# Attention in bursts of three units, value matmuls of 256 queries on all four column tiles

## The chip, the cores and the metric

The kernel runs on one core of one Trainium2 chip. The metric is the device time of one execution in microseconds. The kernel before took 1284.57 us (median of three runs, 1284.06 to 1284.71).

## What is computed

A transformer block on x of shape (4, 1024, 256), in fp32. First attention with 16 heads of 16 channels:

```python
q, k, v = (split_heads(binlinear(layernorm(x), W, b)) for W, b in ((Wq, bq), (Wk, bk), (Wv, bv)))
att = softmax(einsum('bhtd,bhsd->bhts', q, k) * 16 ** -0.5)
y = einsum('bhts,bhsd->bhtd', att, v)
x = x + layernorm(binlinear(y.reshape(B, T, C), Wp, bp))
```

where binlinear multiplies by sign(W) and the mean of |W| over a row. Then a feed-forward part with ternary weights: silu(x w1) * (x w2), two hidden layers of 1024 with gelu, and a last layer back to 256, again with a layer norm and a residual. The change is in the attention alone.

## The kernel before

The program has three stages, each a block in which every engine has its own instruction list: project (queries, keys and values of batch 0), attention, and tail_ffn. The queries, keys and values go through DRAM scratch.

attention goes over four batches. A quad is four heads; a batch has four quads (QUADS_OF_BATCH), and each quad is done in two blocks of 512 queries (BLK), called halves here: 32 halves in all (HALVES). A half has eight turns (ST = 8), one for every 128 keys, so a batch has 64 turns (TURNS_OF_BATCH) and the kernel 256.

In a turn TensorE (block.tensor) does two units, one for each pair of heads. scores(turn), line 1040, writes a unit in two matmuls, one for each head: 50 rows by 128 keys as weights, 512 queries moving, in fp32r. The two lie on different halves of the array's rows. A unit fills one of three PSUM tiles s_ps (two banks each); unit a may be written only when the exp of unit a - 3 is done (line 1051, semaphore probs_ready). ScalarE (line 1202) turns a unit of scores, 128 x 1024, into probs with one exp, line 1210, and signals probs_ready; it needs the semaphore scored for its input and, for the first unit of a turn, pv_done for the buffer (there are 2 x 2 buffers probs). pv(turn), line 1058, multiplies by the values in full fp32: four matmuls, one for each head, each with 17 columns of weights (16 channels and a column of ones, which gives the sum of the softmax), all 512 queries moving, on column tile j of the array (tile_position=(0, 32 * j)). The profile shows a fp32 matmul as two weight loads and two matmul records. All turns of a half accumulate in one bank, y_ps. TensorE's order is scores of turn t, values of turn t - 1, and then, at certain turns, a piece of the next batch's projection.

These pieces are placed by projected(b, t), line 1125. A batch has two windows of 28 turns, from turn 4 and turn 32; r is the turn within a window. At r = 3 and 4 there are four transposes each (turn_x, line 1071), at r = 6, 9, 12 and 15 four matmuls of 512 columns each (project_qk, line 1083, lines 1089 and 1090), at r = 17 and 19 eight of 256 columns each (project_v), at r = 21 four of 512 columns in bf16 (sum_squares), and in the second window two tiny matmuls at r = 23 and 25. All of them go through one bank, p_ps, which VectorE reads. In the last batch prepared(t), line 1174, has two pieces of eight matmuls, two of four transposes and a small one instead. At the start of each batch there is a read of a flag and a branch (lines 1183 to 1188).

At the end of a half VectorE copies y_ps to y_sb (copy_y, line 1231, 512 elements a partition); the first value matmul of the next half waits for it (line 1064). SyncE then stores y_sb with one DMA (store_y, line 878, issued at line 882) and, every second half, issues the loads of the quad after next. The stores' semaphores y_stored are waited for by SyncE, ScalarE and VectorE at the start of tail_ffn. VectorE also does the projection's vector work and checks the feed-forward weights (check_w) in the same list, in turn order.

Of the kernel before, what the change touches and what calls it, by code (L numbers as in the profile page):

```python
# [6 lines left out]
F32 = mybir.dt.float32  # L7
# [3 lines left out]
ACT = mybir.ActivationFunctionType  # L11
# [3 lines left out]
P = 128  # L15
BATCH, SEQ, DIM = 4, 1024, 256
# [3 lines left out]
BLK = 512  # L20
# [5 lines left out]
QUAD = 4  # L26
QUADS = BATCH * HEADS // QUAD
ST = SEQ // P
QROWS = QUAD * HEAD_DIM
VCOLS = HEAD_DIM + 1  # L30
VQUAD = QUAD * VCOLS
HALF = 64
PAIRS = QUAD // 2
STACK = 3 * HEAD_DIM
STACK_M = STACK + 2
ONES_FROM = 32
QUADS_OF_BATCH = HEADS // QUAD
BATCH_BLOCKS = SEQ // BLK
HALVES = QUADS * BATCH_BLOCKS
TURNS_OF_BATCH = QUADS_OF_BATCH * BATCH_BLOCKS * ST  # L40
FIRST_WINDOW, WINDOW = 4, 28
AT_NORM, AT_TURN, AT_QK, AT_V, AT_SUM, AT_TOP, AT_SPREAD = 2, (3, 4), (6, 9, 12, 15), (17, 19), 21, 23, 25
EPS = 1e-5
SCALE = HEAD_DIM ** -0.5
# [667 lines left out]
def attention(nc, const, q_scr, k_scr, v_scr, m_scr, y_scr, ffn_w, w_scr, W, quads, x, tail_in):  # L712
# [6 lines left out]
    q_st, k_st, v_st, loaded, stored = quads.q, quads.k, quads.v, quads.loaded, quads.stored  # L719
# [5 lines left out]
    with ExitStack() as ctx:  # L725
        def sb(name, shape, dt):
            return ctx.enter_context(nc.sbuf_tensor(name, shape, dt))
# [4 lines left out]
        N = QUAD * ST  # L732
        UNITS_OF_BATCH = PAIRS * TURNS_OF_BATCH
        TURNS = BATCH * TURNS_OF_BATCH
# [15 lines left out]
        half = sb("half", [1, 1], F32)  # L750
# [1 line left out]
        shift_col = sb("shift_col", [HEADS, 1], F32)  # L752
        row_bits = sb("row_bits", [P, 1], F32)
        top_bits = sb("top_bits", [1, 1], F32)
        probs = [[sb(f"probs{w}{pp}", [P, 2, BLK], F32) for pp in range(PAIRS)] for w in range(2)]
        y_sb = [sb(f"y_sb{u}", [P, BLK], F32) for u in range(2)]
        qk = [sb(f"pj_qk{u}", [P, BLK], F32) for u in range(2)]
        square = sb("pj_square", [P, QK, BLK], BF16)
# [1 line left out]
        s_ps = [ctx.enter_context(nc.psum_tensor(f"s_ps{i}", [P, 2, BLK], F32)) for i in range(3)]  # L760
        y_ps = ctx.enter_context(nc.psum_tensor("y_ps", [P, BLK], F32))
# [8 lines left out]
        scored = sem("scored")  # L770
        probs_ready = sem("probs_ready")
        pv_done = sem("pv_done")
        y_copied = sem("y_copied")
        y_cleared = sem("y_cleared")
        y_stored = tail_in.y_stored
# [67 lines left out]
        def _(sp):  # L843
# [34 lines left out]
            def store_y(n):  # L878

                g, tb = divmod(n, BATCH_BLOCKS)  # L880
                sp.wait_ge(y_copied, n + 1)
                sp.dma_start(y_scr[g * P:(g + 1) * P, tb * BLK:(tb + 1) * BLK], y_sb[tb][:, :])\
                    .then_inc(y_stored[tb], 16)

            def load_xb(n):

# [57 lines left out]
            for b in range(BATCH):  # L944
# [11 lines left out]
                for t in range(TURNS_OF_BATCH):  # L956
                    turn = b * TURNS_OF_BATCH + t
                    if turn and turn % ST == 0:
                        n = turn // ST - 1
                        store_y(n)  # L960
                        g = n // BATCH_BLOCKS + 2
# [57 lines left out]
        def _(pe):  # L1019
# [17 lines left out]
                pe.wait_ge(mx_loaded[b], 16 * (12 * (QUADS_OF_BATCH + 1) + 2))  # L1037
                pe.wait_ge(mx_split[b], 3 * QUADS_OF_BATCH + 1)

            def scores(turn):  # L1040

                n, s = divmod(turn, ST)
                g, tb = divmod(n, BATCH_BLOCKS)
                u = g % 2
                if s == 0 and tb == 0:
                    pe.wait_ge(loaded[u], 16 * QUAD_LOADS * (g // 2 + 1))
                    pe.wait_ge(m_loaded[u], 16 * 2 * (g // 2 + 1))
                for pp in range(PAIRS):
                    a = PAIRS * turn + pp
                    if a >= 3:  # L1050
                        pe.wait_ge(probs_ready, a - 2)
                    for hh in range(2):
                        rows = slice(hh * HALF, hh * HALF + STACK_M)
                        i = pe.matmul(s_ps[a % 3][:, hh, :], k_st[u][rows, pp, s * P:(s + 1) * P],  # L1054
                                      q_st[u][rows, pp, tb * BLK:(tb + 1) * BLK], start=True, stop=True)
                    i.then_inc(scored, 1)

            def pv(turn):

                n, s = divmod(turn, ST)  # L1060
                g = n // BATCH_BLOCKS
                pe.wait_ge(probs_ready, PAIRS * (turn + 1))
                if s == 0 and n:
                    pe.wait_ge(y_copied, n)
                for j in range(QUAD):
                    i = pe.matmul(y_ps[32 * j:32 * j + VCOLS, :], v_st[g % 2][:, s, VCOLS * j:VCOLS * (j + 1)],  # L1066
                                  probs[turn % 2][j // 2][:, j % 2, :],
                                  start=(s == 0), stop=(s == ST - 1), tile_position=(0, 32 * j))
                i.then_inc(pv_done, 1)

            def turn_x(b, u, n, c):
# [53 lines left out]
            def projected(b, t):  # L1125

                u, r = window(t)
                n = BATCH_BLOCKS * (b - 1) + u
                for c in range(CT):
                    if r == AT_TURN[c]:  # L1130
                        turn_x(b, u, n, c)
                    if r == AT_V[c]:
                        project_v(n, c)
                for m in range(QK):
                    if r == AT_QK[m]:
                        project_qk(n, m)
                if r == AT_SUM:
                    sum_squares(n)
                if u == BATCH_BLOCKS - 1:
                    if r == AT_TOP:  # L1140
                        turn_top(b)
                    if r == AT_SPREAD:
                        spread_bound(b)
# [30 lines left out]
            def prepared(t):  # L1174

                if t in (36, 38):
                    project_y((t - 36) // 2)
                if t in (51, 53):
                    turn_x1((t - 51) // 2)
                if t == 57:  # L1180
                    turn_bits()

            for b in range(BATCH):
                if b:
                    pe.wait_ge(flag_set, b)
                wide = pe.value_load(const.wide_range[:, b:b + 1], min_val=0, max_val=1)
                with pe.If(wide):
                    most_of_rows(b)
                if b == 0:
                    pe.wait_ge(y_cleared, 1)  # L1190
                for t in range(TURNS_OF_BATCH):
                    turn = b * TURNS_OF_BATCH + t
                    scores(turn)
                    if turn:
                        pv(turn - 1)
                    if b + 1 < BATCH:
                        projected(b + 1, t)
                    else:
                        prepared(t)
            pv(TURNS - 1)  # L1200

        @block.scalar
        def _(act):
            for turn in range(TURNS):
                if turn >= 2:
                    act.wait_ge(pv_done, turn - 1)
                for pp in range(PAIRS):
                    a = PAIRS * turn + pp
                    act.wait_ge(scored, a + 1)
                    act.activation(probs[turn % 2][pp][:, :, :], s_ps[a % 3][:, :, :], ACT.Exp,  # L1210
                                   scale=SCALE).then_inc(probs_ready, 1)

        @block.vector
        def _(dve):
# [14 lines left out]
                                      ALU.subtract).then_inc(mx_split[b], 1)  # L1229

            def copy_y(n):
                dve.wait_ge(pv_done, ST * (n + 1))
                if n >= 2:
                    dve.wait_ge(y_stored[n % 2], 16 * (n // 2))
                dve.tensor_copy(y_sb[n % 2][:, :], y_ps[:, :]).then_inc(y_copied, 1)  # L1235

            def check_w(i):
# [164 lines left out]
            for b in range(BATCH):  # L1402
# [5 lines left out]
                for t in range(TURNS_OF_BATCH):  # L1408
                    turn = b * TURNS_OF_BATCH + t
# [13 lines left out]
def tail_ffn(nc, x, y_scr, const, W, tail_in, out):  # L1423
# [9 lines left out]
    with ExitStack() as ctx:  # L1433
        def sb(name, shape, dt):
            return ctx.enter_context(nc.sbuf_tensor(name, shape, dt))
# [110 lines left out]
        @block.sync  # L1546
        def _(sp):
            def load_y(t, b, u):

                sp.wait_ge(y_lo_done, t)  # L1550
                load_tail_y(sp, y_scr, tail_in, b, u)

            def load_x(t, u):
                if not isinstance(t, int) or t >= 2:
                    sp.wait_ge(o_done, t - 1)
                sp.dma_start(x1[u][:, :, :], x_blk[t]).then_inc(x_loaded[u], 16)

            def store(f):
                sp.wait_ge(o_done, f + 1)
                sp.dma_start(o_blk[f], o_sb[:, :, :]).then_inc(o_stored, 16)  # L1560

            def step(i, u, ahead, behind):
                if ahead:
                    load_y(i + 1, *ahead)
                if behind:
                    store(i - 1)
                if ahead:
                    load_x(i + 1, 1 - u)

            for u in range(2):  # L1570
                sp.wait_ge(tail_in.y_stored[u], 16 * HALVES // 2)
            blocks(sp, step, lambda: store(BLOCKS - 1))
            sp.wait_ge(o_stored, 16 * BLOCKS)

# [91 lines left out]
        def _(act):  # L1666
# [54 lines left out]
                ln_std(ln_out(BLOCKS - 1))  # L1721

            for u in range(2):
                act.wait_ge(tail_in.y_stored[u], 16 * HALVES // 2)
            blocks(act, step, end)

        @block.vector
        def _(dve):
# [114 lines left out]
                scale_out(i, ahead)  # L1843

            for u in range(2):
                dve.wait_ge(tail_in.y_stored[u], 16 * HALVES // 2)
            blocks(dve, step, lambda: finish_out(BLOCKS - 1, (BLOCKS - 1) % 2))


# [33 lines left out]
```

## Time and profile before

| | us |
|---|---|
| median of three runs | 1284.57 |
| lowest, highest | 1284.06, 1284.71 |
| the profiled execution, whole | 1285.64 |
| its span, first to last instruction | 1283.9 |
| TensorE busy (share of the span) | 1193.3 (93%) |
| ScalarE busy | 726.2 (57%) |
| VectorE busy | 631.1 (49%) |
| attention, first exp start to last exp start | 65.2 to 593.8 |
| granted TensorE clock, mean share | 0.983 |

The span is divided into the start and the projection of batch 0 (to 65 us), attention (to 598), and the feed-forward part (to 1283.9). Busy means that some instruction of the engine was under way. A matmul's record begins when it starts to stream and ends about 165 ns after its columns have gone through, so that records overlap and TensorE looks busy where it is only draining.

### The profile page before, as it was taken

What the parts mean: (1) busy time and instruction counts of PE and PEld (TensorE: products, weight loads), DVE (VectorE), ACT (ScalarE), POOL (GpSimd) and SP (SyncE); (2) the same over time, 40 slices, a digit from 0 to 9 for tenths busy, and PEclk for the clock granted to TensorE, in tenths of its full rate; (3) what the DMA queues carried; (4) which work ended last, traced back from release to release, by engine and by line L of the source; (5) the groups of instructions that cost most, each with busy time, mean ns of one, the idle gap of its engine ahead of it and who ended that gap; (6) DMA issues with size and microseconds to landing.
All of it is one profiled execution on the core that took longest, in us unless ns stands there. A gap on an engine that the chain in (4) does not pass through costs nothing.

```text
span 1283.9 us, 17482 instructions
## 1 busy us (share of the span) xinstructions
PE 1193.3 (93%) x6705; PEld 727.1 (57%) x6705; DVE 631.1 (49%) x1150; ACT 726.2 (57%) x866; POOL 78.6 (6%) x78
## 2 busy tenths in 40 slices
PE   3299989999999999998999999999999999999997
PEld 3123222323232322224888888888888888888886
DVE  6234433444353431442656747646577376575523
ACT  4288979898989899997324224233242342432411
POOL 5101110111011100000000000000000000000000
PEclk9689999999999999999999999999999999999999
DMA  3868567776765678512010201001001010010000
GB/s 114 225 175 229 132 158 160 181 183 165 153 173 158 195 162 156 89 33 66 1 34 1 66 1 34 33 1 41 26 14 53 1 34 33 1 33 1 17 1 17
DMA packets 52712, 107.55 MB, mean 84 GB/s; under 512 B 6544, under 2 KB 23312, under 8 KB 52620
## 3 DMA queue, kind: packets, MB, share of 16 engines
q1 hardware_dynamic: 52332, 105.54, 32.5%
q10 hardware_dynamic: 288, 0.79, 0.5%
q8 instruction: 57, 0.93, 0.3%
q14 instruction: 35, 0.29, 0.1%
HBM read 71.94 MB, written 45.88 MB: 92 GB/s over the span
## 4 chain that ended last, share of the span: by engine, by line
PE 53%; DVE 0%; issue 0%; ACT 0%; POOLq 0%; DVEq 0%
PE ffn_ps L1601 23%; PE ffn_ps L1600 23%; PE ffn_ps L1628 2%; PE ffn_ps L1629 2%; PE side_ps L1584 1%; PE side_ps L1593 0%; DVE ln_stats L1731 0%; DVE zn L1742 0%; DVE zn L1783 0%; DVE zn L1793 0%; DVE ln_mean_var L1735 0%; ACT ln_std L1669 0%; DVE ln_rstd L1739 0%; POOLq L1538 0%; DVEq L1781 0%
## 5 line engine op out<-in xcount | busy, mean ns | idle before, releaser
L1210 ACT ACTIVATE probs<-s_ps 128x1024 f32<-128x1024 f32 x512 | 477.0, 1054 | 71.9 <-PE s_ps L1054 71.6
L1601 PE MATMUL ffn_ps<-h_lo,W 128*128 128x512 f32 x1024 | 405.9, 396 | 0.0
L1600 PE MATMUL ffn_ps<-h_hi,W 128*128 128x512 f32 x1024 | 403.0, 394 | 0.0
L1066 PE MATMUL y_ps<-probs,v_st 128*17 128x512 f32 x2048 | 272.0, 603 | 34.1 <-ACT probs L1210 17.2
L1601 PEld LDWEIGHTS ffn_ps<-h_lo,W 128*128 128x128 f32 x1024 | 192.0, 188 | 47.5
L1600 PEld LDWEIGHTS ffn_ps<-h_hi,W 128*128 128x128 f32 x1024 | 191.9, 187 | 45.7
L1690 ACT ACTIVATE hid<-ffn_ps,scales 128x512 f32<-128x512 f32 x128 | 80.9, 685 | 240.0 <-PE ffn_ps L1601 235.0
L1054 PE MATMUL s_ps<-q_st,k_st 50*128 50x512 f32 x1024 | 190.0, 449 | 20.3 <-DMA q_st<-shift 19.6
L1054 PEld LDWEIGHTS s_ps<-q_st,k_st 50*128 50x128 f32 x1024 | 77.5, 187 | 200.4 <-ACT probs L1210 163.1
L1807 DVE CAST h_hi<-hid 128x512 fp32r<-128x512 f32 x128 | 53.4, 417 | 192.8 <-ACT hid L1690 192.7
L1801 DVE TENSOR_TENSOR h_lo<-hid,h_hi 128x512 fp32r<-128x512 f32 x192 | 130.0, 684 | 1.1
L1066 PEld LDWEIGHTS y_ps<-probs,v_st 128*17 128x17 f32 x2048 | 34.7, 95 | 141.3 <-ACT probs L1210 120.0
L1600 PE MATMUL ffn_ps<-x_hi,W 128*128 128x512 f32 x256 | 100.7, 393 | 2.7 <-POOLq L1538 2.7
L1601 PE MATMUL ffn_ps<-x_lo,W 128*128 128x512 f32 x256 | 100.4, 392 | 0.0
L1235 DVE COPY y_sb<-y_ps 128x512 f32<-128x512 f32 x32 | 22.1, 690 | 145.7 <-PE y_ps L1066 145.7
L1815 DVE SCALAR_TENSOR_TENSOR hid<-ffn_ps,scales,gate 128x512 f32<-128x512 f32 x64 | 47.5, 750 | 43.7 <-ACT gate L1701 26.3
L1701 ACT ACTIVATE gate<-ffn_ps,scales 128x512 f32<-128x512 f32 x64 | 43.3, 687 | 32.8 <-PE ffn_ps L1601 32.8
L1628 PE MATMUL ffn_ps<-W,h_hi 128*128 128x256 f32 x256 | 61.6, 283 | 0.0
L1629 PE MATMUL ffn_ps<-W,h_lo 128*128 128x256 f32 x256 | 61.0, 281 | 0.0
L1669 ACT ACTIVATE ln_std<-ln_mean_var,eps 128x4 f32<-128x4 f32 x22 | 6.5, 298 | 88.0 <-DVE ln_mean_var L1735 88.0
L1600 PEld LDWEIGHTS ffn_ps<-x_hi,W 128*128 128x128 f32 x256 | 48.6, 190 | 13.5 <-POOLq L1538 3.6
L142 DVE RECIPROCAL sums<-sums 128x256 f32<-128x256 f32 x32 | 54.5, 1730 | 0.0
(156 smaller groups left out, 944.8 us busy)
## 6 DMA issues: line engine op xcount, KB each, us to landing
q_st<-q_scr SPq DMA_DIRECT2D x96, 128.0 KB, 7.4
k_st<-k_scr SPq DMA_DIRECT2D x90, 128.0 KB, 4.6
w_scr<-ffn_w SPq DMA_DIRECT2D x16, 704.0 KB, 7.8
W<-w_scr SPq DMA_DIRECT2D x16, 704.0 KB, 6.2
y_scr<-y_sb SPq DMA_DIRECT2D x32, 256.0 KB, 2.2
v_st<-v_scr SPq DMA_DIRECT2D x16, 272.0 KB, 8.7
y<-y_scr SPq DMA_DIRECT2D x16, 256.0 KB
sums<-y_scr SPq DMA_DIRECT2D x16, 256.0 KB
```

What stands on the lines that cost most here:

```text
L142: dve.reciprocal(sums, sums).then_inc(tail_in.inverted, 1)
L1054: i = pe.matmul(s_ps[a % 3][:, hh, :], k_st[u][rows, pp, s * P:(s + 1) * P], q_st[u][rows, pp, tb * BLK:(tb + 1) * BLK], start=True, stop= ...
L1066: i = pe.matmul(y_ps[32 * j:32 * j + VCOLS, :], v_st[g % 2][:, s, VCOLS * j:VCOLS * (j + 1)], probs[turn % 2][j // 2][:, j % 2, :], start= ...
L1210: act.activation(probs[turn % 2][pp][:, :, :], s_ps[a % 3][:, :, :], ACT.Exp, scale=SCALE).then_inc(probs_ready, 1)
L1600: pe.matmul(bank_of(t)[:, :], w, hi[:, k, :].bitcast(form), start=(k == 0), stop=False)
L1601: mm = pe.matmul(bank_of(t)[:, :], w, lo[:, k, :].bitcast(form), start=False, stop=last)
L1628: pe.matmul(dst, hi[:, k, tokens].bitcast(form), w, start=(k == 0 and a == 0), stop=False)
L1629: mm = pe.matmul(dst, lo[:, k, tokens].bitcast(form), w, start=False, stop=(k == HT - 1 and a == per_bank - 1))
L1690: act.activation(hid[n % 3][:, :], bank_of(t)[:, :], ACT.Gelu, scale=scales[:, s:s + 1]).then_inc(gelu_done, 1)
L1801: dve.tensor_tensor(h_lo[a][:, n, :], hid[n % 3][:, :], h_hi[a][:, n, :].bitcast(F32), ALU.subtract).then_inc(h_lo_done, 1)
L1807: dve.tensor_copy(h_hi[a][:, n, :], hid[n % 3][:, :]).then_inc(hi2_done, 1)
L1815: dve.scalar_tensor_tensor(hid[n % 3][:, :], bank_of(2 * n + 1)[:, :], scales[:, S2_AT + n:S2_AT + n + 1], gate[n % 3][:, :], ALU.mult, AL ...
```

## The change

Units are counted through, without regard to turns. A half has 16 units, in bursts of 3, 3, 3, 3, 2 and 2. TensorE's order is now: scores of a burst, values of the burst before it, and then the pieces of projection of every turn that this burst's scores complete. pv takes one unit: a head's 512 queries are split in two halves of 256, and the four pairs of head and query half lie on the four column tiles. So y_ps has another layout: rows are head of the pair and query half, columns are the pair and 256 queries; one y_sb needs four stores to keep the layout in DRAM. There are five buffers probs, one for each unit, in place of four. ScalarE waits for pv_done and scored at every unit.

```diff
+BURSTS = (3, 3, 3, 3, 2, 2)
+UNITS_OF_HALF = 2 * ST
+PROBS = 5
+QH = BLK // 2
...
-                sp.dma_start(y_scr[g * P:(g + 1) * P, tb * BLK:(tb + 1) * BLK], y_sb[tb][:, :])\
-                    .then_inc(y_stored[tb], 16)
+                for j in range(2):
+                    for h in range(2):
+                        c = 32 * (2 * j + h)
+                        sp.dma_start(rows[j, h], y_sb[tb][c:c + 32, :].rearrange("d (pp q) -> d pp q", pp=PAIRS))\
+                            .then_inc(y_stored[tb], 16)
...
-                pe.wait_ge(probs_ready, PAIRS * (turn + 1))
-                if s == 0 and n:
+                pe.wait_ge(probs_ready, a + 1)
+                if s == 0 and pp == 0 and n:
                     pe.wait_ge(y_copied, n)
-                for j in range(QUAD):
-                    i = pe.matmul(y_ps[32 * j:32 * j + VCOLS, :], v_st[g % 2][:, s, VCOLS * j:VCOLS * (j + 1)],
-                                  probs[turn % 2][j // 2][:, j % 2, :],
-                                  start=(s == 0), stop=(s == ST - 1), tile_position=(0, 32 * j))
+                for c in range(QUAD):
+                    j, h = divmod(c, 2)
+                    head = PAIRS * pp + j
+                    i = pe.matmul(y_ps[32 * c:32 * c + VCOLS, pp * QH:(pp + 1) * QH],
+                                  v_st[g % 2][:, s, VCOLS * head:VCOLS * (head + 1)],
+                                  probs[a % PROBS][:, j, h * QH:(h + 1) * QH],
+                                  start=(s == 0 and pp == 0), stop=(s == ST - 1 and pp == PAIRS - 1), tile_position=(0, 32 * c))
...
+                for half in range(QUADS_OF_BATCH * BATCH_BLOCKS):
+                    for k, size in enumerate(BURSTS):
+                        a = b * UNITS_OF_BATCH + half * UNITS_OF_HALF + sum(BURSTS[:k])
+                        for i in range(a, a + size):
+                            scores(i)
+                        for i in range(max(a - BURSTS[k - 1], 0), a):
+                            pv(i)
+                        while t < TURNS_OF_BATCH and PAIRS * (b * TURNS_OF_BATCH + t + 1) <= a + size:
+                            if b + 1 < BATCH:
+                                projected(b + 1, t)
+                            else:
+                                prepared(t)
+                            t += 1
...
+            for a in range(PAIRS * TURNS):
+                if a >= PROBS:
+                    act.wait_ge(pv_done, a - PROBS + 1)
+                act.wait_ge(scored, a + 1)
+                act.activation(probs[a % PROBS][:, :, :], s_ps[a % 3][:, :, :], ACT.Exp, scale=SCALE)\
+                    .then_inc(probs_ready, 1)
```

The waits on y_stored in tail_ffn and in copy_y count four stores a half. VectorE's and GpSimd's lists are otherwise as before.

## Rows read from the trace of the kernel before

**Rows 1.** The page: busy time of each engine over the whole span.

```profile
PE 1193.3 (93%) x6705; PEld 727.1 (57%) x6705; DVE 631.1 (49%) x1150; ACT 726.2 (57%) x866; POOL 78.6 (6%) x78
```

**Rows 2.** Stretches (batches 0, 1, 3, end): busy PE, PEld, DVE, ACT, POOL; clock, DMA, GB/s.

```profile
65.00:204.80 139.80, 130.14 (x855) 40.50 (x851) 51.38 (x87) 119.82 (x129) 17.68 (x15) 0.96 0.66 170
204.80:339.40 134.60, 126.35 (x861) 39.75 (x860) 57.27 (x96) 119.57 (x129) 18.18 (x15) 1.00 0.72 174
...
474.00:594.00 120.00, 112.21 (x790) 30.38 (x789) 36.45 (x62) 117.18 (x128) 2.43 (x4) 1.00 0.46 85
594.00:598.60 4.60, 1.22 (x12) 0.13 (x8) 0.69 (x1) 0.89 (x1) 0.00 (x0) 0.97 0.15 57
```

**Rows 3.** The page: costliest groups by line (busy us, mean ns, idle before).

```profile
L1210 ACT ACTIVATE probs<-s_ps 128x1024 f32<-128x1024 f32 x512 | 477.0, 1054 | 71.9 <-PE s_ps L1054 71.6
L1066 PE MATMUL y_ps<-probs,v_st 128*17 128x512 f32 x2048 | 272.0, 603 | 34.1 <-ACT probs L1210 17.2
```

**Rows 4.** Waits, 60 to 598 us: waiter, waited for, total us, times, longest.

```profile
ACT probs L1210 <- PE s_ps L1054: 71.6, 61, 19.2
```

**Rows 5.** Timeline of a turn without projection: start us, length us, engine, line.

```profile
589.89 0.61 PE L1066 MATMUL y_ps<-probs,v_st 128*17 128x512 f32 x4
590.43 0.73 PE L1054 MATMUL s_ps<-q_st,k_st 50*128 50x512 f32 x4
591.28 1.05 PE L1066 MATMUL y_ps<-probs,v_st 128*17 128x512 f32 x8
```

**Rows 6.** Timeline of ScalarE alone: the last twelve exps, and one of them.

```profile
583.79 11.10 ACT L1210 ACTIVATE probs<-s_ps 128x1024 f32<-128x1024 f32 x12
...
589.23 1.08 ACT L1210 ACTIVATE probs<-s_ps 128x1024 f32<-128x1024 f32 x1
```

**Rows 7.** Timeline around one project_qk in batch 1.

```profile
302.07 2.88 ACT L1210 ACTIVATE probs<-s_ps 128x1024 f32<-128x1024 f32 x3
...
303.17 1.05 PE L1066 MATMUL y_ps<-probs,v_st 128*17 128x512 f32 x8
...
304.15 0.50 PE L1089 MATMUL p_ps<-x_hi,signs 128*128 128x512 f32 x1
...
304.95 0.40 PE L1090 MATMUL p_ps<-x_lo,signs 128*128 128x512 f32 x1
...
305.28 0.73 PE L1054 MATMUL s_ps<-q_st,k_st 50*128 50x512 f32 x4
...
305.89 1.02 ACT L1210 ACTIVATE probs<-s_ps 128x1024 f32<-128x1024 f32 x1 [0.94 <-PE s_ps L1054]
...
305.94 1.05 PE L1066 MATMUL y_ps<-probs,v_st 128*17 128x512 f32 x7
```

**Rows 8.** Timeline of 2 ns, 337.550 to 337.552 us: what of a pv had started.

```profile
337.54 0.11 PEld L1066 LDWEIGHTS y_ps<-probs,v_st 128*17 128x17 f32 x4 [0.55 <-ACT probs L1210]
337.54 0.62 PE L1066 MATMUL y_ps<-probs,v_st 128*17 128x512 f32 x3
```

**Rows 9.** Timeline after the branch at the start of batch 2.

```profile
338.71 0.33 PEld L1054 LDWEIGHTS s_ps<-q_st,k_st 50*128 50x128 f32 x4 [1.04 <-issue]
...
339.40 0.13 PEld L1066 LDWEIGHTS y_ps<-probs,v_st 128*17 128x17 f32 x8 [0.36 <-ACT probs L1210]
```

**Rows 10.** Timelines of VectorE and TensorE at the latest copy of batch 1.

```profile
308.03 0.68 DVE L1235 COPY y_sb<-y_ps 128x512 f32<-128x512 f32 x1
...
308.85 1.05 PE L1066 MATMUL y_ps<-probs,v_st 128*17 128x512 f32 x8 [1.20 <-ACT probs L1210]
```

**Rows 11.** Timeline of the end of attention.

```profile
594.95 1.05 PE L1066 MATMUL y_ps<-probs,v_st 128*17 128x512 f32 x8 [0.78 <-ACT probs L1210]
...
596.78 0.33 SPq L882 DMA_DIRECT2D y_scr<-y_sb  x1
```

**Rows 12.** Timeline of SyncE's queue: two stores issued in a row.

```profile
301.59 0.33 SPq L896 DMA_DIRECT2D k_scr<-y  x1
301.97 0.43 SPq L896 DMA_DIRECT2D k_scr<-sums  x1
```

More of the change, by code:

```diff
@@ L754, in attention @@
         top_bits = sb("top_bits", [1, 1], F32)
-        probs = [[sb(f"probs{w}{pp}", [P, 2, BLK], F32) for pp in range(PAIRS)] for w in range(2)]
+        probs = [sb(f"probs{i}", [P, 2, BLK], F32) for i in range(PROBS)]
         y_sb = [sb(f"y_sb{u}", [P, BLK], F32) for u in range(2)]
@@ L881, in store_y @@
                 sp.wait_ge(y_copied, n + 1)
-                sp.dma_start(y_scr[g * P:(g + 1) * P, tb * BLK:(tb + 1) * BLK], y_sb[tb][:, :])\
-                    .then_inc(y_stored[tb], 16)
+                rows = y_scr[g * P:(g + 1) * P, tb * BLK:(tb + 1) * BLK].rearrange("(pp j d) (h q) -> j h d pp q", pp=PAIRS,
+                                                                                   j=2, h=2)
+                for j in range(2):
[3 more added lines that the diff above has]
+                            .then_inc(y_stored[tb], 16)
             def load_xb(n):
@@ L1038, in most_of_rows, with scores @@
                 pe.wait_ge(mx_split[b], 3 * QUADS_OF_BATCH + 1)
-            def scores(turn):
-                n, s = divmod(turn, ST)
+            def scores(a):
+                n, s = divmod(a // PAIRS, ST)
+                pp = a % PAIRS
                 g, tb = divmod(n, BATCH_BLOCKS)
                 u = g % 2
-                if s == 0 and tb == 0:
+                if s == 0 and tb == 0 and pp == 0:
                     pe.wait_ge(loaded[u], 16 * QUAD_LOADS * (g // 2 + 1))
                     pe.wait_ge(m_loaded[u], 16 * 2 * (g // 2 + 1))
[L1048 to L1056, printed above, removed]
@@ L1058, in pv @@
-            def pv(turn):
-                n, s = divmod(turn, ST)
+                if a >= 3:
+                    pe.wait_ge(probs_ready, a - 2)
+                for hh in range(2):
+                    rows = slice(hh * HALF, hh * HALF + STACK_M)
+                    i = pe.matmul(s_ps[a % 3][:, hh, :], k_st[u][rows, pp, s * P:(s + 1) * P],
+                                  q_st[u][rows, pp, tb * BLK:(tb + 1) * BLK], start=True, stop=True)
+                i.then_inc(scored, 1)
+            def pv(a):
+                n, s = divmod(a // PAIRS, ST)
+                pp = a % PAIRS
@@ L1190, in _ @@
                     pe.wait_ge(y_cleared, 1)
[L1191 to L1200, printed above, removed]
+                t = 0
+                for half in range(QUADS_OF_BATCH * BATCH_BLOCKS):
[11 more added lines that the diff above has]
+                            t += 1
+            for i in range(PAIRS * TURNS - BURSTS[-1], PAIRS * TURNS):
+                pv(i)
         @block.scalar
         def _(act):
[L1204 to L1211, printed above, removed]
+            for a in range(PAIRS * TURNS):
[4 more added lines that the diff above has]
+                    .then_inc(probs_ready, 1)
         @block.vector
@@ L1231, in copy_y @@
             def copy_y(n):
-                dve.wait_ge(pv_done, ST * (n + 1))
+                dve.wait_ge(pv_done, UNITS_OF_HALF * (n + 1))
                 if n >= 2:
-                    dve.wait_ge(y_stored[n % 2], 16 * (n // 2))
+                    dve.wait_ge(y_stored[n % 2], 16 * QUAD * (n // 2))
                 dve.tensor_copy(y_sb[n % 2][:, :], y_ps[:, :]).then_inc(y_copied, 1)
@@ L1570, in _ @@
             for u in range(2):
-                sp.wait_ge(tail_in.y_stored[u], 16 * HALVES // 2)
+                sp.wait_ge(tail_in.y_stored[u], 16 * QUAD * HALVES // 2)
             blocks(sp, step, lambda: store(BLOCKS - 1))
@@ L1723, in _ @@
             for u in range(2):
-                act.wait_ge(tail_in.y_stored[u], 16 * HALVES // 2)
+                act.wait_ge(tail_in.y_stored[u], 16 * QUAD * HALVES // 2)
             blocks(act, step, end)
@@ L1845, in _ @@
             for u in range(2):
-                dve.wait_ge(tail_in.y_stored[u], 16 * HALVES // 2)
+                dve.wait_ge(tail_in.y_stored[u], 16 * QUAD * HALVES // 2)
             blocks(dve, step, lambda: finish_out(BLOCKS - 1, (BLOCKS - 1) % 2))
```

## The prediction, made before the changed kernel ran

> **What bounds the kernel now.** I read the busy times first [rows 1], then the stretches [rows 2]: the change can only act in attention, 65 to 598 us, 42% of the span. There TensorE looks busiest, but its records overlap while it drains; ScalarE is the engine to follow. In batch 3, which has few pieces of projection, ScalarE is busy 117.2 of 120.0 us; in batch 1 it is busy 119.6 of 134.6 [rows 2]. Its floor: the last twelve exps end at 594.89 and the one that starts at 589.23 ends at 590.31, so the five behind it took 4.58, a pitch of 0.916 us [rows 6]; 16 units (a half) 14.66, 128 units (a batch) 117.3. Batch 1 loses 17.3 us above that floor, batch 0 about 22, batch 3 about 3. The waits name the cause: ScalarE waited for scores 61 times, 71.6 us, 19.2 of them before the first exp [rows 3, 4].
>
> Why it waits is a chain. From the end of a turn's second exp: 0.05 to the value matmuls [rows 6, 11]; 0.98 to TensorE's next work, of which 0.44 is the first group of four (1.05 less 0.61), 0.54 the second with the switch [rows 5, 7]; 0.61 to the start of the exp; 1.02 for it [rows 7]. That is 2.66, and ScalarE allows three pitches, 2.75: 0.09 of slack. A project_qk lies between 304.15 and 305.28, 1.13 us, and the next exp ends 1.96 after the one before it instead of 0.92: 1.04 is lost, 1.13 less the slack [rows 7]. So nearly the whole of each piece of projection becomes idle time of ScalarE, though TensorE itself needs only 0.66 + 0.98 = 1.64 of a turn's 1.83 [rows 7].
>
> **The durations of the changed order.** A score unit streams 0.23: the four projection matmuls start 0.80 apart in all, the first pitch 0.34 with its weight load open (0.73 less 0.40 gives it too), the others 0.23 [rows 7]. From the second unit to the values it is 0.66 - 0.34 = 0.32. So three units of scores take 0.34 + 0.23 + 0.32 = 0.89, two 0.66. A value group streams 0.427 (0.44 less 0.013 for the first load); a unit of 256 queries is two groups of half that, 0.427 again, with the switch and first load 0.13 once for a burst: 1.41 for three units, 0.98 for two. That no time is lost between one unit's groups and the next's the trace of before never shows, as a tile there has two groups and no more. The bounds are nothing, and the nearest price of an opened load and switch, 0.09 (0.32 less 0.23). I take nothing: the second group's loads start in the shadow of the first's stream, and within 10 ns four loads and three matmuls had begun [rows 8], so that a load held back lets those of the other tiles pass; from the second unit on there are 0.21 us of stream to hide a load in.
>
> TensorE's pace by bursts is then 0.89 + 0.98 = 1.87 (first), 2.30 (second to fourth), 0.66 + 1.41 = 2.07 (fifth), 1.64 (sixth); ScalarE's 2.75 four times and 1.83 twice. Over a half that is 12.5 against 13.1 before: two pairs of switches fewer.
>
> **The sum.** Where a chain binds, the steps from the end of an exp are: burst of three after three, 0.05 + 0.43 (last score unit with its load) + 1.41 + 0.61 + 1.02 = 3.52 against four pitches 3.67, slack 0.15. First after the sixth: 0.43 less, slack 0.58. To the sixth burst (unit 14) from unit 8: 0.05 + 0.43 + 1.41 + 0.66 + 1.40 + 0.61 + 1.02 = 5.58 against six pitches 5.50: it comes 0.07 to 0.09 late in every quiet half, a cost of the change of 32 x 0.07 = 2.2.
>
> A piece of 1.13 (project_qk; project_v is as long) lost 1.04 before. After: 0.54 behind the first burst; 0.97 behind the second and third; behind the fourth 0.97 and again 0.22 at unit 14 (2.07 against 1.83); 0.68 in place of 0.97 where it comes one burst after another piece, since nothing waits any more and the pace counts (2.30 + 1.13 - 2.75); 1.35 behind the fifth; 0.92 behind the sixth. Turn t of eight lies at burst 1 (t = 0), 2 (1, 2), 3 (3), 4 (4, 5), 5 (6), 6 (7). For the twelve pieces at turns 10, 13, 16, 19, 21, 23, 38, 41, 44, 47, 49 and 51 this gives 0.97 + 1.19 + 0.54 + 0.97 + 0.89 + 0.93 + 1.35 + 0.97 + 1.19 + 0.92 + 0.97 + 0.67 = 11.6 against 12.5: -0.9 for a batch. The first pair of transposes lost 0.9 and loses 0.44, as one falls behind the first burst; the second pair 0.9 and 0.8; the two sums of squares 1.5 and 1.3; the small matmuls 0.26 and 0.10: another -0.9. (Laid out unit by unit with these durations, attention before comes to 528.1 from first to last exp, where the trace has 528.6.)
>
> Then the copy of y. Before, the first value matmul of a half has it barely in time, and where VectorE is behind with the projection it waits: copy at 308.03, values at 308.85 after 1.20 idle [rows 10]. I put that at 1.0 for this half, 1.8 for one half of batch 0, and 0.03 to 0.2 for the others: 1.1 in batches 1 and 2. After, three more score units lie ahead of it: from the end of the exp of unit 15, 0.05 + 0.43 + 0.98 + 0.24 + 0.68 + 0.07 = 2.45 to the copy's end, and the matmul is due at 2.75 + 0.05 + 0.43 = 3.23, 0.8 of slack. All but 0.5 in batch 0 and 0.5 in batch 2 goes.
>
> Batch 1: -0.9 - 0.9 - 1.1 + 0.2 (its quiet halves) = -2.7. Batch 2: -2.3. Batch 0: -4.1, and -1.0 for its late copy, after which part of the clock's 4% shortfall [rows 2] falls, which the shorter wait should spare. Batch 3: 0.3 of late copies saved, 0.5 of late sixth bursts added: +0.2. Attention: -9.9.
>
> The end: three more stores are issued between the copy and the end of SyncE's list, 0.38 each [rows 12]: +1.1 (the first issue stands at 596.78 [rows 11]); but behind the last exp only one value unit of 0.54 is left instead of 0.98 [rows 11]: -0.4. Elsewhere the 31 x 3 extra issues lie in SyncE's list ahead of quad loads that are due a half or more later (14.7 us): nothing; without that cover 1.1 for each half with loads, 14 in all. ScalarE's extra waits are for pv(a - 5), done in the burst before: unit a + 2 of a burst wants the first value unit of the last one, ready 0.5 ahead. Nothing. TensorE's value instructions double to 16 a unit; its list must deliver 60 in 2.30 us, 38 ns each. After the branch, with an empty list, 20 (four loads, four matmuls, then eight loads and the four matmuls beside them) were there within 0.73 us, waits included [rows 9], so at most 36 ns each: nothing, but close.
>
> Sum, on the profiled execution (1285.64, span 1283.9) and equally on the median 1.1 below it: -9.9 + 0.7 = -9.2; 1284.57 - 9.2 = 1275.4.
>
> **Rules of the skill.** The rows show 0.11 of switch from values to scores (0.54 less 0.43) [rows 5]. The Trainium skill (TensorEngine Tiling (Array Packing), Key Properties) says that a change of tiling mode drains TensorE, which is why fewer changes should pay; row and rule agree. Against the change: the rows show loads of the same four tiles beginning while matmuls stream [rows 8]. The Trainium skill (TensorE: Matmul & The Clock Gate, Part 3, The mechanism) says that loads overlap matmuls in flight only where their row groups differ; here all four tiles take all rows, so by it every group would wait for its load. The trace speaks against it for two groups; for the third it can't.
>
> **Rivals.** *Loads come into the open between units.* 0.09 for every unit but a burst's first, 320 in all. In the bursts of three this turns 0.15 of slack into -0.03, and the way to unit 14, which has none, takes 0.37 more; with the losses at insertions 0.56 a half, 18 in all: 1293.4. It decides from about 0.05 a unit, where the gain is gone. If every group pays, 5 x 0.09 in a burst of three, less its slack, 1.2 a half, 39 in all: 1314. For it: no tile ever had a third group. Against it: rows 8. Chances 0.13 and 0.08.
>
> *The list of TensorE is too slow.* At 55 ns an instruction, half again the bound of rows 9, a burst of three takes 3.3 against 2.75, +20% in 469 us (512 exps): 1370. Against it rows 9. Chance 0.04.
>
> *The switches are saved and the time isn't.* The score unit that must wait still opens its load, each value group costs its 0.013, the slack is then what it was, and the late unit 14 is 0.2 later (32 x 0.2 = 6.4): -9.9 + 6.4 + 0.7 = -2.8, 1281.8. Half of its 0.17 lies on either side of the bound below.
>
> *More comes back than slack.* The pieces are spread by TensorE's spare time of 0.6 us a half, 32 x 0.6 = 20 at most: 1265. Chance 0.03.
>
> **How the numbers follow.** My forecast, 1275.4 (own range 1270 to 1280.5), has 0.55. The range to 1294 takes in the small gain and the milder rival, and leaves out the two dear ones and the tails; the low end is 1268. A difference under 0.2% (2.6 us) can't be told from none by these measurements. Faster: 0.55 + 0.08 + 0.03 = 0.66; within: 0.09; slower: 0.13 + 0.08 + 0.04 = 0.25.
>
> **What would show it.** Right: the exps at 0.916 in quiet halves with one 0.98 to 1.0 at unit 14; value groups 0.21 apart right through a burst; a lone project_qk costing 0.97 behind the second burst and 0.54 behind the first; batch 1 near 132; the last exp near 584. Wrong: a step of 0.3 instead of 0.21 between a unit's last group and the next unit's first; groups of a tile starting staggered; ScalarE waiting for probs buffers; the passage to the feed-forward part longer than 5.5 us.

## The result and the profile after

The changed kernel takes 1288.9 us (median; the kernel before, run beside it, 1284.8): a ratio of 1.0028, with a 95% interval of 1.0018 to 1.0038. It is slower by 0.3%, where 1275.4 us was forecast, 0.7% faster. The profiled execution took 1291.6 us with a span of 1289.8, 5.9 above that of before. Inside the batches the forecast gain comes, as the runs below show; at three places that the prediction never looked at, the starts of batches 1 to 3, it is all given back and more.

The page of the changed kernel, busy times and groups as in [rows 1, 3]:

```profile
PE 1195.0 (93%) x8753; PEld 803.9 (62%) x8753; DVE 631.0 (49%) x1150; ACT 728.8 (57%) x866; POOL 78.6 (6%) x78
...
L1226 ACT ACTIVATE probs<-s_ps 128x1024 f32<-128x1024 f32 x512 | 479.5, 1051 | 74.3 <-PE s_ps L1062 72.1
...
L1077 PE MATMUL y_ps<-probs,v_st 128*17 128x256 f32 x4096 | 263.6, 387 | 0.7 <-DVE y_sb L1251 0.4
```

TensorE's idle time before value matmuls fell from 34.1 us, of which 17.2 were waits for exps [rows 3], to 0.7. The waiting for exps is not gone: it stands before the score matmuls now, 24.8 us where it was 0.3. It costs nothing in itself, since ScalarE sets the pace. But ScalarE waits for scores as long as before, 72.1 us, and the waits say what is new in that. Those of the changed kernel, 60 to 604 us, columns as in [rows 4]:

```profile
ACT probs L1226 <- PE s_ps L1062: 72.1, 62, 18.8
...
PE s_ps L1062 <- ACT probs L1226: 24.8, 82, 0.4
...
PE s_ps L1062 <- DMA q_st<-m_scr: 11.9, 3, 4.8
```

TensorE waits three times, 11.9 us in all, for the load of rows from m_scr into q_st. Of the 71.6 us in [rows 4], 19.2 came before the first exp, and most of the rest were pieces of projection. Here 12 us are something else. The stretches by batch (columns as in [rows 2]; the bounds follow the changed kernel's own batches) show where:

```profile
65.00:204.00 139.00, 127.63 (x1359) 59.36 (x1355) 51.36 (x87) 120.40 (x129) 17.68 (x15) 0.97 0.70 172
204.00:339.60 135.60, 127.18 (x1374) 59.16 (x1371) 57.30 (x96) 120.10 (x129) 18.18 (x15) 0.98 0.71 173
339.60:477.40 137.80, 126.68 (x1375) 59.06 (x1371) 57.30 (x96) 120.17 (x129) 18.18 (x15) 0.98 0.69 167
477.40:600.00 122.60, 115.40 (x1315) 49.33 (x1315) 36.45 (x62) 118.72 (x128) 2.44 (x4) 0.98 0.47 83
```

Batch 1 takes 135.6 in place of 134.6, batch 3 122.6 in place of about 121; and the granted clock, 1.00 in batches 1 and 3 before [rows 2], is 0.98. One passage from a batch to the next, batch 0 to 1, is enough to see both. The timeline of the changed kernel (start us, length us, engine, line):

```profile
187.34 2.44 SPq L891 DMA_DIRECT2D y_scr<-y_sb  x4
...
188.88 0.20 PE L1135 MATMUL p_ps<-pj_bound,pj_ones 1*16 1x1 f32 x2
...
189.29 0.68 DVE L1339 CAST shift<-shift_col 16x1024 fp32r<-16x1024 f32 x1
...
191.33 0.34 SPq L178 DMA_DIRECT2D v_st<-v_scr  x1
191.72 0.43 SPq L877 DMA_DIRECT2D W<-w_scr  x1
192.20 0.52 SPq L872 DMA_DIRECT2D w_scr<-ffn_w  x1
...
192.76 0.58 SPq L915 DMA_DIRECT2D m_scr<-shift  x1
...
197.10 1.06 PE L1077 MATMUL y_ps<-probs,v_st 128*17 128x256 f32 x16
200.56 0.56 SPq L852 DMA_DIRECT2D q_st<-m_scr  x2
...
202.93 1.65 PE L1062 MATMUL s_ps<-q_st,k_st 50*128 50x512 f32 x6 [4.76 <-DMA q_st<-m_scr]
```

A batch's shift (a constant taken off the scores so that the exp can't overflow) is made at turn 57 of the batch before: a small matmul at 188.88, ready in SBUF at 189.97. It goes to DRAM and comes back as two rows of the first quad's query tile. Its store is issued at 192.76, behind four stores of y, a load of values that waits until the values are stored, and a piece of the feed-forward weights, 704 KB out and 704 KB in. It lands at 200.56, when SyncE goes on to the loads; these land at 202.9. TensorE had ended the batch's last values at about 198.2 and stood for 4.8 us. The same list in the kernel before:

```profile
191.00 0.43 SPq L174 DMA_DIRECT2D v_st<-v_scr  x1
191.47 0.46 SPq L873 DMA_DIRECT2D W<-w_scr  x1
191.97 0.50 SPq L868 DMA_DIRECT2D w_scr<-ffn_w  x1
192.81 0.98 SPq L906 DMA_DIRECT2D m_scr<-shift  x1
198.73 0.56 SPq L848 DMA_DIRECT2D q_st<-m_scr  x2
```

There the store landed at 198.73; with 2.4 for the loads as above (an estimate) the rows were in place at 201.1, and the next batch's scores came at 204.15. Three us of slack stood there that no view shows as a wait. The changed kernel comes 5.7 us earlier to this place and its store lands 1.8 later.

At the three passages ScalarE loses 4.9, 2.4 and 5.0 us, 12.3 together, reckoned as the distance between the ends of a batch's last exp and of the next batch's first, less the pitch of 0.916. These three are called the stalls from here on.

Around the end of each stall, and for some us behind it, TensorE runs at half its clock (1.2 of 2.4 GHz). A part of that stretch at the first stall, with the clock as the third number from the end:

```profile
203.00:206.80 3.80, 3.80 (x24) 1.74 (x26) 0.32 (x1) 2.85 (x3) 0.00 (x0) 0.50 0.00 0
```

### The profile page after: what moved, and what is told of

Read it like the earlier page. It is cut to its first block, busy times and chain, and to the rows that moved or that the text cites. A ratio compares the mean times of both kernels' runs of the same rounds, so it can differ in the third digit from the quotient of the medians.

```text
span 1289.8 us, 21927 instructions
## 1 busy us (share of the span) xinstructions
PE 1195.0 (93%) x8753; PEld 803.9 (62%) x8753; DVE 631.0 (49%) x1150; ACT 728.8 (57%) x866; POOL 78.6 (6%) x78
## 4 chain that ended last, share of the span: by engine, by line
PE 52%; DVE 0%; issue 0%; ACT 0%; POOLq 0%; DVEq 0%
PE ffn_ps L1617 23%; PE ffn_ps L1616 23%; PE ffn_ps L1644 2%; PE ffn_ps L1645 2%; PE side_ps L1600 1%; PE side_ps L1609 0%; DVE ln_stats L1747 0%; DVE zn L1758 0%; DVE zn L1799 0%; DVE zn L1809 0%; DVE ln_mean_var L1751 0%; ACT ln_std L1685 0%; DVE ln_rstd L1755 0%; POOLq L1554 0%; DVEq L1797 0%
## 5 line engine op out<-in xcount | busy, mean ns | idle before, releaser
L1226 ACT ACTIVATE probs<-s_ps 128x1024 f32<-128x1024 f32 x512 | 479.5, 1051 | 74.3 <-PE s_ps L1062 72.1
L1077 PE MATMUL y_ps<-probs,v_st 128*17 128x256 f32 x4096 | 263.6, 387 | 0.7 <-DVE y_sb L1251 0.4
L1062 PE MATMUL s_ps<-q_st,k_st 50*128 50x512 f32 x1024 | 203.8, 466 | 56.7 <-ACT probs L1226 24.8
L1062 PEld LDWEIGHTS s_ps<-q_st,k_st 50*128 50x128 f32 x1024 | 87.0, 190 | 169.4 <-ACT probs L1226 105.7
L1077 PEld LDWEIGHTS y_ps<-probs,v_st 128*17 128x17 f32 x4096 | 101.7, 98 | 128.2 <-issue 51.2
L1617 PEld LDWEIGHTS ffn_ps<-x_lo,W 128*128 128x128 f32 x256 | 48.6, 190 | 10.0
```

The costliest lines, as they stand in the source:

```text
L1077: i = pe.matmul(y_ps[32 * c:32 * c + VCOLS, pp * QH:(pp + 1) * QH], v_st[g % 2][:, s, VCOLS * head:VCOLS * (head + 1)], probs[a % PROBS][: ...
L1226: act.activation(probs[a % PROBS][:, :, :], s_ps[a % 3][:, :, :], ACT.Exp, scale=SCALE)\
L1617: mm = pe.matmul(bank_of(t)[:, :], w, lo[:, k, :].bitcast(form), start=False, stop=last)
```

## What was run to settle it

Every ratio below is to the kernel before as it ran beside the run in question. Its median was 1285.8 us beside e1 to e4 and again beside e5 to e8, 1284.8 beside the changed kernel; so a difference of 1 or 2 us between absolute times from different groups says little.

**The wait taken out (e1).** The first quad of a batch takes the shift rows of the batch before, which lie in DRAM long since, and loads them early. The softmax doesn't change with the shift as long as nothing overflows. What this kernel leaves out is each batch's own shift for its first quad. (Not shown below: load_shift itself, which now takes as a third argument the quad whose rows it reads.)

```diff
...
@@ def load_first_quad(b)
                 load_stacks(sp, q_scr, k_scr, q_st[0], k_st[0], b * QUADS_OF_BATCH, loaded[0])
+                load_shift(b * QUADS_OF_BATCH, m_loaded[0], (b - 1) * QUADS_OF_BATCH)
@@ def projected(b, t)
                     if r == AT_SPREAD + 2:
                         store_shift(b)
-                        sp.wait_ge(shift_stored, 16 * (b + 1))
-                        load_shift(b * QUADS_OF_BATCH, m_loaded[0])
@@ the loop over turns
                             load_quad(sp, q_scr, k_scr, v_scr, quads, g, g % 2)
+                            sp.wait_ge(shift_stored, 16 * (g // QUADS_OF_BATCH + 1))
                             load_shift(g, m_loaded[g % 2])
```

> The changed kernel, but the shift rows of a batch's first quad are not the ones computed for that batch: they are loaded early from the rows of the batch before (the softmax doesn't depend on the shift as long as nothing overflows), so that no wait for the shift's way through DRAM stands at the start of a batch. Theory A (the bursts gain what was forecast inside the batches, and the starts of batches 1 to 3 give it back, since the loads of the shift rows now end last): the three stalls of 4.9, 2.4 and 5.0 us before a batch's first exp go, and most of the 3.0 us that TensorE loses at its half clock behind them, together 12 to 15 us: 1274 to 1277, a ratio to the kernel before of 0.992 to 0.994. Theory B (the batches' starts wait for something else too, the quad's queries, keys and values or the rest of the queue): the stalls shrink by less than half, 1283 or more.

Measured: 1277.3 us, 0.9948 of the kernel before (0.993 to 0.9965), 11.6 under the changed kernel (10.3 by the two ratios). Theory A gave 1274 to 1277, of which this is 0.3 short; theory B's 1283 is out. No wait for m_scr is left, and ScalarE's waits for scores are 14 us shorter:

```profile
ACT probs L1227 <- PE s_ps L1063: 58.1, 55, 18.7
```

**The same edit on the kernel before (e2).**

> The kernel before with the same edit (a batch's first quad takes the shift rows of the batch before, loaded early). Theory A: before, the shift rows landed some 3 us ahead of TensorE, so nothing is won: within 1 us of the kernel before. Theory B, if the shift's way cost the kernel before something as well, by the traffic at the end of a batch: 3 us or more faster.

Measured: 1284.7, a ratio of 0.9994 (0.9976 to 1.0011). As theory A has it: before the change this way through DRAM cost nothing that shows (the interval reaches from 3 us faster to 1.4 slower). The stall isn't a fault of the kernel before that the change merely failed to mend; the change turned slack into a wait.

**What held the store back (e4).** Each batch's own shift again, and only the order in SyncE's list changed: weights behind shift.

```diff
-                    if turn % 13 == 4 and turn // 13 < QUADS:
-                        load_w(turn // 13)
+                    late = TURNS_OF_BATCH - 2
+                    due = [i for i in range(QUADS) if (13 * i + 4 == turn and t < 54)
+                           or (t == late and turn - late + 54 <= 13 * i + 4 <= turn + 1)]
+                    for i in due:
+                        load_w(i)
```

> The changed kernel with one thing moved: the copy of a piece of the feed-forward weights (704 KB to DRAM scratch and 704 KB from it) that SyncE issues just ahead of the store of the shift rows, at turns 56 to 58 of a batch, is issued at turn 62, behind the loads of the shift rows. Theory A in its sharper form (the shift rows are late because their store lies behind those 1.4 MB in the DMA queues): the store lands some 2 to 3 us after its issue in place of 7.8, the stalls at the starts of batches fall to under 1 us each, 1276 to 1280. If the lateness comes from SyncE's order instead (the four stores of y and the wait for the stored values ahead of it): the stalls shrink by 2 us at most, 1284 or more.

Measured: 1277.05, a ratio of 0.9943 (0.9922 to 0.9965): as good as leaving the wait out. SyncE's list at the same passage:

```profile
190.56 0.34 SPq L178 DMA_DIRECT2D v_st<-v_scr  x1
190.95 0.43 SPq L915 DMA_DIRECT2D m_scr<-shift  x1
193.62 0.56 SPq L852 DMA_DIRECT2D q_st<-m_scr  x2
194.23 0.35 SPq L877 DMA_DIRECT2D W<-w_scr  x1
```

The store is issued 1.8 earlier and lands after 2.7 us in place of 7.8 (192.76 to 200.56); at the other two passages after 2.6 and 2.9 in place of 6.5 and 8.1. So putting the 1.4 MB behind the store is enough to end all three stalls, as the sharper form of theory A has it. That nothing else has a part in them doesn't follow; see e8. The stretches of e4, batches 1 and 3:

```profile
198.30:330.30 132.00, 125.54 (x1372) 58.29 (x1371) 57.29 (x96) 119.88 (x129) 18.16 (x15) 1.00 0.75 180
...
462.50:583.90 121.40, 113.97 (x1311) 48.81 (x1309) 36.45 (x62) 118.64 (x129) 2.43 (x4) 1.00 0.49 93
```

The clock is back at 1.00, and batch 1 takes 132.0: the prediction's -2.7 against 134.6 [rows 2] gave 131.9. From the start of one batch's first exp to that of the next (to the last exp's end for batch 3), e4's batches 0 to 3 differ from those of the kernel before by -5.6, -2.6, -2.3 and +0.4 us, where -5.1, -2.7, -2.3 and +0.2 were forecast: -10.0 in all, where -9.9 was forecast. The last exp starts at 582.9, where 584 was forecast (attention itself began 1.0 earlier in this run).

**The four stores of y (e8).** One store in place of four, with the weights where they were. What this kernel leaves out is the right order of rows, so its output is permuted.

```diff
-                for j in range(2):
-                    for h in range(2):
-                        c = 32 * (2 * j + h)
-                        sp.dma_start(rows[j, h], y_sb[tb][c:c + 32, :].rearrange("d (pp q) -> d pp q", pp=PAIRS))\
-                            .then_inc(y_stored[tb], 16)
+                sp.dma_start(y_scr[g * P:(g + 1) * P, tb * BLK:(tb + 1) * BLK], y_sb[tb][:, :])\
+                    .then_inc(y_stored[tb], 16)
```

> The changed kernel with one store of y for a half in place of four; the rows land in another order than the later loads expect, so the attention output is permuted, with the same bytes and loads. If the three more issues and the smaller pieces held back the shift's way at the end of a batch: the stalls of 4.9, 2.4 and 5.0 us shrink by 1 us or more each, 1282 to 1285. If they lie beside the wait for the stored values, as the order in SyncE's list suggests: only the 0.8 to 1.1 us at the end of attention go, 1287 to 1288.

Measured: 1283.9, a ratio of 0.9988 (0.9976 to 1.0), 5 under the changed kernel. The time is in the first answer's range, and I had leaned to the other. But not each stall shrinks by 1 us: those at the first two passages fall from 4.9 and 2.4 us to 0.5 and none, the third only from 5.0 to 4.6. SyncE's list at the third:

```profile
451.65 0.36 SPq L886 DMA_DIRECT2D y_scr<-y_sb  x1
457.44 0.33 SPq L178 DMA_DIRECT2D v_st<-v_scr  x1
457.81 0.43 SPq L877 DMA_DIRECT2D W<-w_scr  x1
458.28 0.50 SPq L872 DMA_DIRECT2D w_scr<-ffn_w  x1
458.82 0.59 SPq L910 DMA_DIRECT2D m_scr<-shift  x1
465.51 0.56 SPq L852 DMA_DIRECT2D q_st<-m_scr  x2
```

Between 452.0 and 457.4 it waits until the stored values have landed, with the shift's store, whose data was ready at 455.1, behind it. So the small stores have a part in the first two stalls, but they are not needed for a stall.

Their part is not the time that they take in SyncE's list. In the changed kernel that is 1.76 to 3.12 us at the three passages, and each time SyncE then stands another 1.5 to 2.0 us until the stored values have landed, which covers it. What differs in e8 is how soon things land: at the first two passages the values 8.9 and 7.6 us after their issue in place of 10.3 and 9.3, and the shift's store after 6.1 and 4.8 in place of 7.8 and 6.5. That the small pieces slow the transfers in flight beside them would fit; it was not shown by itself, and at the third passage the values took longer in e8, 11.1 in place of 9.6.

**The value split by itself (e6), and with the weights moved (e5) or the shift early (e3).** Bursts of two throughout: the order of units of the kernel before, with values of 256 queries.

```diff
-BURSTS = (3, 3, 3, 3, 2, 2)
+BURSTS = (2,) * 8
```

> The changed kernel with early shift rows and bursts of two units throughout (2,2,2,2,2,2,2,2) in place of (3,3,3,3,2,2): the value matmuls of 256 queries without the bursts of three. By the durations of the prediction: two units of scores 0.66, values of the two before 0.98, the same 1.64 as a turn of the kernel before, but the last score unit of a burst waits for nothing that the values must follow, and the first value unit needs only its own exp: from the end of the exp before, 0.05 + 0.43 + 0.12 + 0.61 + 1.02 = 2.23 against three pitches 2.75, a slack of 0.5 where it was 0.09. Insertions of 1.13 then cost 0.6 to 0.9: attention 18 to 19 us shorter than before, 1265 to 1269. The rival, that fewer switches of tiles are what gains: slower than the bursts of three with the same edit, 1276 or more.

Measured e3: 1268.7, a ratio of 0.988 (0.9861 to 0.9899), in the range of the theory, under the rival's 1276, and 8.6 under the bursts of three with the same edit (e1). Attention alone is 17.3 us shorter than before, a little less than the 18 to 19 worked out.

> The changed kernel with bursts of two units throughout and, as in e4, the copy of a piece of the feed-forward weights issued behind the loads of the shift rows instead of ahead of their store; each batch uses its own shift rows. Theory A (the end of the shift's way is all that held the starts of batches, and bursts of two have the larger slack): as e3, 1268 to 1270. If e3's gain came from leaving out the wait itself and not from its being early enough: 2 us or more above e3.

Measured e5: 1268.7, a ratio of 0.9865 (0.9846 to 0.9883), the same as e3. It leaves nothing of the computation out, and it beats both kernels. The kernel before with the weights moved was not run; e2, which takes the wait out of it altogether, gained nothing. Nor was the split of the values run without the fifth buffer probs; in the kernel before 71.6 of ScalarE's 71.9 idle us in attention were waits for scores [rows 3, 4], so that buffers did not bind there. Around a project_qk, and batch 1:

```profile
225.79 0.50 PE L1104 MATMUL p_ps<-x_hi,signs 128*128 128x512 f32 x1
...
226.92 0.73 PE L1065 MATMUL s_ps<-q_st,k_st 50*128 50x512 f32 x4
...
227.52 2.85 ACT L1229 ACTIVATE probs<-s_ps 128x1024 f32<-128x1024 f32 x3 [0.51 <-PE s_ps L1065]
```
```profile
200.00:329.40 129.40, 126.62 (x1373) 54.52 (x1371) 57.28 (x96) 119.27 (x128) 18.18 (x15) 1.00 0.74 181
```

The piece is as long as ever, 1.13, and ScalarE idles 0.51 for it where it idled 0.94 [rows 7]. Before, all values of a turn waited for its second exp, and the scores stood behind them. With one value unit for each exp, only half of the values does.

> The changed kernel with bursts of two units throughout and nothing else: the value matmuls of 256 queries by themselves, in the order of units that the kernel before had. The matmul that starts the shift's way through DRAM then stands two units earlier in the batch than with the bursts of three, as in the kernel before, 12 us ahead of the next batch's first scores instead of 9. Theory A with the slack of 3 us at the batches' starts as a matter of order: stalls of under 2 us each instead of 4.9, 2.4 and 5.0, 1270 to 1276. If the stalls come with the earlier arrival alone: the batches end another 2.5 us earlier each, so the stalls grow to 5 and more, 1281 to 1287.

Measured e6: 1277.3, a ratio of 0.993 (0.991 to 0.9949), just outside the first theory's 1270 to 1276, and clearly not the second's. The stalls are 0.2, 1.3 and 5.3 us: at two of the three passages they are under 2 us, as the first theory has it (that the earlier place of the shift's first matmul does this is argued, not shown by itself); at the third SyncE waits for stored values until 451.7, as in e8. Neither expectation had that. The waits of e6:

```profile
PE s_ps L1062 <- DMA q_st<-m_scr: 7.2, 2, 5.5
```

**The order of the sizes (e7).** With the weights moved as in e4.

```diff
-BURSTS = (3, 3, 3, 3, 2, 2)
+BURSTS = (3, 3, 3, 2, 3, 2)
```

> As e4, with the six bursts of a half in the order 3, 3, 3, 2, 3, 2 instead of 3, 3, 3, 3, 2, 2. The fifth burst's pace of 2.07 against 1.83 was the step without slack: a burst of two behind threes whose values are three units. Laid out with the prediction's durations, this order takes 3.8 us less in attention: 1273 to 1274. If the order of sizes doesn't matter (the sum of TensorE's work in a half is the same, 12.5 us): 1277.

Measured: 1272.8, a ratio of 0.9902 (0.9885 to 0.9919), 0.2 under the range, and 4.2 under e4; 3.8 was worked out. As e4 belongs to the other group of runs, the two profiles are the better comparison: attention takes 515.5 us in e7, 519.8 in e4, 4.3 less. The step without slack that the prediction put behind the fourth burst is real, and it can be moved.

## Why the prediction was wrong, point by point

*The bound and the chain* were right: the time inside batches follows the slack of the chain from an exp through values and scores to the next exp. Without the stalls (e4) batch 1 took 132.0 against 131.9 and attention was 10.0 us shorter against 9.9, and e3, e5 and e7, forecast from the same durations, came in their ranges or within 0.2 us of them.

*The value groups* were taken without a price between units, against a rival of 0.09. In the changed kernel, around the same project_qk of batch 1:

```profile
225.06 0.50 PE L1101 MATMUL p_ps<-x_hi,signs 128*128 128x512 f32 x1
...
226.19 0.96 PE L1062 MATMUL s_ps<-q_st,k_st 50*128 50x512 f32 x6
226.80 2.86 ACT L1226 ACTIVATE probs<-s_ps 128x1024 f32<-128x1024 f32 x3 [0.88 <-PE s_ps L1062]
227.08 1.49 PE L1077 MATMUL y_ps<-probs,v_st 128*17 128x256 f32 x24
```

Three units of values are six groups of four records; less 0.38 for the last record, all 24 start within 1.11 us. By the starts of single records the sixth group starts 1.09 after the first: 0.227 to the second, with the first load, and 0.216 each from there on, 0.002 above the 0.2135 assumed, also where one unit ends and the next begins. With the milder rival's price it would be 1.27. The measured 1288.9 lies nearer to that rival's 1293.4 than to the forecast, but doesn't come from it. ScalarE's next exp ends 0.99 late behind the second burst; 0.97 was forecast. The trace speaks against the rule of the Trainium skill that loads overlap matmuls only where row groups differ (TensorE: Matmul & The Clock Gate, Part 3, The mechanism), for these column tiles: all take all rows, and the 0.216 leaves no room for a load in the open. The same section also lets a load go ahead of matmuls in flight when it targets the background weight buffer; that would fit, but no view here shows which buffer a load takes.

*The list of TensorE* kept up: 24 loads and 24 matmuls of such a burst began within those 1.11 us.

*The late unit 14* came 0.10 to 0.12 late in quiet halves, by the ends of the single exps; 0.07 was worked out. Right in kind, and some 1.3 us short over the kernel's 32 halves. As attention without the stalls came to -10.0 against -9.9, other terms were off by about as much the other way; which, no run separates. That the sum came so close is in part luck.

*The end* was forecast at +0.7. The timeline:

```profile
598.79 1.02 ACT L1226 ACTIVATE probs<-s_ps 128x1024 f32<-128x1024 f32 x1
...
601.27 1.75 SPq L891 DMA_DIRECT2D y_scr<-y_sb  x4
...
604.40 0.49 PE L1616 MATMUL ffn_ps<-x_hi,W 128*128 128x512 f32 x1 [3.92 <-POOLq L1554]
```

From the last exp's end, 599.81, to the feed-forward part 4.59 us, against 3.77 (594.89 to 598.66): +0.8.

*The step that failed* is the sentence that elsewhere the extra issues lie in SyncE's list ahead of quad loads due a half or more later: nothing. It looked at the stores' cost and at the loads of quads, and passed over the one round trip that isn't due a half later, the shift: made at turn 57, due at turn 64. It also failed to ask the converse: what, if TensorE comes 5.7 us earlier, is not there yet. The runs show both in place of that nothing: without the wait (e1) 11.6 us come back, the same edit gives the kernel before nothing (e2), and with one store in place of four (e8) two of the three stalls go and 5 us come back. How the rest divides between the earlier arrival and the stores was not separated. The sum lacked three stalls of 4.9, 2.4 and 5.0 us, 12.3 together, and 3.0 for the half clock behind them (the first halves of batches 1 to 3 are 1.3, 0.6 and 1.1 longer than in e4). With these the forecast for the profiled execution, -9.2, becomes +6.1; it was +5.9.

*The forecast of 1275.4 against e4's 1277.05*: part of the difference is the other group of runs, where the kernel before took 1285.8 and not 1284.6. By the profiles e4's span is 8.8 us shorter than before (1275.1 against 1283.9), where 9.2 was forecast: -1.0 before attention, -10.0 in it, +0.7 at its end and +1.4 in the feed-forward part (686.7 against 685.3), where the clock is halved for 6.8 us around its start instead of 3.4.

## What to carry to other kernels

When a change makes the bounding loop faster, list every transfer and flag that the loop meets at its seams and reckon its slack, not its wait: a transfer with 3 us to spare looks like nothing in a profile and ends last when the loop gains 5. A tiny store on a critical round trip belongs ahead of bulk copies (e4). And before bursts are made longer to save switches, reckon the chain: with the finer value units, bursts of two (e3, e5) were 8 us better than bursts of three (e1, e4), though they save no switch; the gain came from the shorter chain.

## What the runs showed of the hardware that was not expected

A store of 64 KB issued behind 1.4 MB landed after 6.5 to 8.1 us at the changed kernel's three passages, the same store ahead of them (e4) after 2.6 to 2.9. Four stores of 64 KB from 32 partitions each took 1.74 to 4.02 us of SyncE's list (median 1.76) where one of 256 KB took 0.33 to 1.17 (median 0.34). A TensorE stall of 4.8 us is followed by a stretch at half clock (0.50 from 203.0 to 206.8), so that the three stalls here cost about a quarter more than their length (3.0 us on 12.3). Why the store behind the same 1.4 MB landed after 5.6 to 6.2 us before and after 6.5 to 8.1 in the changed kernel was not settled; the y stores in smaller pieces just ahead are the likely cause, as it took 4.8 to 6.7 with one store (e8) and 6.5 to 8.0 with four in e6.
